# Level 3 of a wavelet convolution with fewer matmuls, up-sampling with high and low halves stacked, and the residual sum earlier on VectorE

## The reference

```python
x = x + _L0_conv_ref(_gn(x), w_qkv, w_proj, gamma, beta)
x = x + _L1_conv_ref(_gn(x), base_w, base_b, base_scale, wconv_w, wscale)

def _L1_conv_ref(x, base_w, base_b, base_scale, wconv_w, wscale):
    cur = x
    for i in range(3):                 # WT_LEVELS
        co = haar2d(cur)               # 4 coefficient planes at half the size
        cur = co[:, :, 0]
        flat = dwconv(co.reshape(B, C * 4, h, w), wconv_w[i]) * wscale[i]   # 5 x 5 depthwise
        level_coeffs.append(flat.reshape(B, C, 4, h, w))
    next_ll = zeros_like(level_coeffs[-1][:, :, 0])
    for i in reversed(range(3)):
        co = level_coeffs[i].at[:, :, 0].add(next_ll)
        next_ll = ihaar2d(co)          # twice the size
    return dwconv(x, base_w) * base_scale + base_b + next_ll
```

## Time and profile before

| | |
|---|---|
| time, median of 3 runs | 11314.09 us (11312.22 to 11319.58) |
| the profiled execution | 11311.75 us, of which its span 11309.9 us |
| PE busy | 10853.3 us (96%) |
| DVE busy | 9314.2 us (82%) |
| ACT busy | 6979.7 us (62%) |
| POOL busy | 3419.9 us (30%) |
| mean granted TensorE clock | 0.992 of full speed |

### The profile page before, as it was taken

One profiled execution on the slowest core, in us unless ns is written; L12 is line 12 of the kernel. 1 busy time (PEld: TensorE's weight loads), 2 busy tenths in 40 slices (PEclk: granted clock), 3 DMA queues, 4 the chain that ended last, 5 costly groups with the idle time before them and its releaser, 6 DMA issues.

```text
span 11309.9 us, 208798 instructions
## 1 busy us (share of the span) xinstructions
PE 10853.3 (96%) x68772; PEld 9284.1 (82%) x68772; DVE 9314.2 (82%) x16092; ACT 6979.7 (62%) x11660; POOL 3419.9 (30%) x2756
## 2 busy tenths in 40 slices
PE   4999999999999999999599999999999999999999
PEld 4888888888888888888588888888888888888888
DVE  6989999899998989988677777777777777777777
ACT  4777777777777777788445445454454545545454
POOL 3444444344444444444222122212222122221221
PEclk9999999999999999999799999999999999999999
DMA  5333233233333333222266666666666766667665
GB/s 184 126 101 125 96 123 123 92 129 101 114 114 116 113 101 130 93 80 81 73 140 151 148 148 147 145 153 147 149 145 145 154 146 150 144 146 153 145 150 118
DMA packets 1149039, 1453.41 MB, mean 129 GB/s; under 512 B 201567, under 2 KB 1111199, under 8 KB 1111455
## 3 DMA queue, kind: packets, MB, share of 16 engines
q1 hardware_dynamic: 1147231, 1442.74, 50.1%
q10 hardware_dynamic: 1376, 6.13, 0.1%
HBM read 1040.06 MB, written 408.56 MB: 128 GB/s over the span
## 4 chain that ended last, share of the span: by engine, by line
PE 49%; DVE 1%; SPq 0%; DMA 0%; issue 0%; POOL 0%; DVEq 0%; POOLq 0%
PE ps_w L1274 10%; PE ps_w L1275 10%; PE ps_w L1276 10%; PE ps_ll L1282 4%; PE ps L1274 4%; PE ps L1275 4%; PE ps L1276 4%; PE ps_w L1317 4%; DVE ob L1399 0%; DVE x L1337 0%; DMA yb<-y_scratch 0%; SPq L1101 0%; SPq L1110 0%; DMA prm<-params 0%; SPq L1120 0%
## 5 line engine op out<-in xcount | busy, mean ns | idle before, releaser
L1274 PE MATMUL ps_w<-zb,mat 128*128 128x512 f32 x4800 | 1925.7, 401 | 1.6 <-DVE ob L1399 1.6
L1276 PE MATMUL ps_w<-zb,mat 128*128 128x512 f32 x4800 | 1907.6, 397 | 0.0
L1275 PE MATMUL ps_w<-zb,mat 128*128 128x512 f32 x4800 | 1907.2, 397 | 0.0
L1227 ACT ACTIVATE z<-x,prm 64x384 f32<-64x384 f32 (+1 forms) x3072 | 1807.2, 659 | 55.5 <-DVE x L1337 47.8
L635 POOL CAST xn_hi<-xs 96x512 fp32r<-96x512 f32 x1024 | 842.7, 823 | 3106.9 <-PE ps_qkv L660 2255.4
L1173 POOL CAST mat<-raw 128x1280 fp32r<-128x1280 f32 (+1 forms) x288 | 344.8, 1215 | 4454.8 <-DMA raw<-vec 2674.2
L1399 DVE SCALAR_TENSOR_TENSOR ob<-ps_w,prm,x 64x512 f32<-64x512 f32 x1920 | 1440.6, 750 | 148.7 <-PE ps_w L1317 109.5
L1337 DVE SCALAR_TENSOR_TENSOR x<-yb,prm,xb 128x1024 f32<-128x1024 f32 (+1 forms) x576 | 1120.4, 1997 | 421.6 <-DMA prm<-params 374.9
L658 PE MATMUL ps_qkv<-wqkv_hi,xn_hi 96*128 96x288 f32 x4096 | 1388.4, 339 | 38.0 <-POOL xn_lo L637 19.8
L637 POOL TENSOR_TENSOR xn_lo<-xs,xn_hi 96x512 fp32r<-96x512 f32 x1024 | 1363.7, 1332 | 81.9
L1247 ACT ACTIVATE ll<-ps_ll 128x512 f32<-128x512 f32 x192 | 115.1, 599 | 1880.5 <-PE ps_ll L1282 1880.5
(11 more groups left out here) (183 smaller groups left out, 24815.2 us busy)
## 6 DMA issues: line engine op xcount, KB each, us to landing
xst<-in_x SPq DMA_DIRECT2D x96, 2048.0 KB, 13.8
xs<-in_x SPq DMA_DIRECT2D x128, 1536.0 KB, 8.9
y_scratch<-ys SPq DMA_DIRECT2D x128, 1536.0 KB, 9.5
out<-ob SPq DMA_DIRECT2D x768, 208.0 KB
xb<-in_x SPq DMA_DIRECT2D x576, 256.0 KB
yb<-y_scratch SPq DMA_DIRECT2D x576, 256.0 KB
raw<-vec SPq DMA_DIRECT2D x192, 320.0 KB, 5.4
raw<-vec SPq DMA_DIRECT2D x384, 160.0 KB, 4.2
```

Source lines behind the costliest of these rows:

```text
L1227: last = nc.scalar.activation(z[q * WROWS:(q + 1) * WROWS, ts, b, :], x1[slot(k, g)][rows, pairs, b, q::2], ACT.Identity, scale=prm[k][row ...
L1274: mm(out_, w[HI], xx[HI], start=start, stop=False)
L1275: mm(out_, w[HI], xx[LO], start=False, stop=False)
L1276: return mm(out_, w[LO], xx[HI], start=False, stop=stop)
```

## The change

- Level 3 on PE: the high and the low part of its input lie side by side in one tensor `in3_hl`. One matmul with the high weights takes both (256 columns, into both halves of `ps_3[:, s]`), a second one with the low weights takes the high part (128 columns). It is 20 matmuls instead of 30. ACT then copies all of `ps_3` (512 columns, not 128) and DVE adds the two halves (`sum3`) ahead of `up3`, whose inputs lie both in SBUF now.
- Up-sampling on PE: the high and the low part of `next_ll` lie on top of each other over the 128 partitions, `next_a` for the upper 64 rows and `next_b` for the lower. Windows 0 and 1 need `next_a` alone, 3 and 4 `next_b` alone, window 2 both: 6 matmuls instead of 10. ACT and DVE write each part in two instructions of 64 partitions.
- `make_x1` stands ahead of `trailing` on DVE.
- The factor of `make_x1` comes from a tensor of its own, `gain`, loaded by a DMA of its own behind the loads of a channel's first set. `prm` is loaded ahead of `raw` on SP; ACT `norm` and DVE `finish` wait for it.
- In the earlier stages three small tensors are given back sooner; nothing that runs there changes.

```diff
@@ wavelet stage, SyncE
+                def load_gain(c, k):
+                    sp.dma_start(gain[k][:], bass.AP(tensor=par_dram.tensor, offset=c * NPAR, ap=[[0, 128], [1, 1]])
+                                 ).then_inc(gain_in[k], 16)
-                def group(m, k, g, fetch=True):
+                def group(m, k, g, fetch=True, more=True):
                     if fetch:
                         m3, k3, g3 = ahead(m, k, g, 3)
                         sp.wait_ge(x1_ready, m * (4 * PAIRW) + (2 * k + g + 3) * PAIRW)
                         sp.sem_inc(sp_turn, 1)
                         load(m3 * 2 + k3, g3)
+                        if g == 0 and more:
+                            load_gain(m * 2 + (k + 2), k)
                     store(m * 2 + k, g, m * 4 + (2 * k + g))
...
                         for g in range(SETS):
                             group(m, k, g)
-                            if g == 1:
-                                sp.wait_ge(mat23_ready, m * 2 + (k + 2))
-                                load_raw(m * 2 + (k + 2))
                         load_prm(m * 2 + (k + 2), k)
+                        sp.wait_ge(mat23_ready, m * 2 + (k + 2))
+                        load_raw(m * 2 + (k + 2))
@@ ScalarE
                     act.wait_ge(l3_ready, qn + 1)
-                    nc.scalar.activation(s3[:], ps_3[:, 0, 0:IMGS * HALF // 4], ACT.Copy).then_inc(s3_copied, 1)
+                    nc.scalar.activation(s3[:].rearrange("p s h n -> p (s h n)"), ps_3[:].rearrange("p s n -> p (s n)"),
+                                         ACT.Copy).then_inc(s3_copied, 1)
                     act.wait_ge(next_ready, qn + 1)
-                    nc.scalar.activation(next_p[HI][:], next_ll[:].rearrange("p n c -> p (n c)"), ACT.Copy
-                                         ).then_inc(next_hi, 1)
+                    both = next_ll[:].rearrange("p n c -> p (n c)")
+                    nc.scalar.activation(next_a[0:64, :], both[0:64], ACT.Copy).then_inc(next_hi, 1)
+                    nc.scalar.activation(next_b[64:128, :], both[64:128], ACT.Copy).then_inc(next_hi, 1)
@@ TensorE
-                    level(ps_3, mat3, in3_p, HALF // 4).then_inc(l3_ready, 1)
+                    for s in range(2):
+                        for d in range(TAPS):
+                            both = (ps_3[:, s, :], mat3[HI][:, s, d, :], in3_hl[:, :, s, :, d:d + HALF // 4])
+                            high = (ps_3[:, s, 0:IMGS * HALF // 4], mat3[LO][:, s, d, :],
+                                    in3_hl[:, HI, s, :, d:d + HALF // 4])
+                            if d == TAPS - 1:
+                                mm(*high, start=False, stop=False)
+                            last = mm(*both, start=d == 0, stop=d == TAPS - 1)
+                            if d < TAPS - 1:
+                                mm(*high, start=False, stop=False)
+                    last.then_inc(l3_ready, 1)
...
                     for t in range(WINDOWS):
-                        for h in (HI, LO):
-                            last = mm(ps_w[t][:], up_sb[:, t, :], next_p[h][:], start=False, stop=h == LO)
+                        upper, lower = t < UPPER, t >= WINDOWS - LOWER
+                        if upper:
+                            last = mm(ps_w[t][:], up_sb[:, t, :], next_a[:], start=False, stop=not lower)
+                        if lower:
+                            last = mm(ps_w[t][:], up_sb[:, UPPER + t - (WINDOWS - LOWER), :], next_b[:], start=False,
+                                      stop=True)
                         last.then_inc(win_ready, 1)
@@ VectorE
                     dve.wait_ge(s3_copied, qn + 1)
-                    v.tensor_tensor(up3[:, :, 0], s3[:], ps_3[:, 1, 0:n], ALU.add)
+                    v.tensor_tensor(sum3[:], s3[:, :, 0], s3[:, :, 1], ALU.add).then_inc(s3_summed, 1)
+                    dve.wait_ge(s3_summed, qn + 1)
+                    v.tensor_tensor(up3[:, :, 0], sum3[:, 0], sum3[:, 1], ALU.add)
...
+                    v.tensor_tensor(next_a[64:128, :], both[0:64], next_a[0:64, :].bitcast(F32), ALU.subtract)
+                    dve.wait_ge(next_hi, qn * 2 + 2)
+                    v.tensor_tensor(next_b[0:64, :], both[64:128], next_b[64:128, :].bitcast(F32), ALU.subtract
+                                    ).then_inc(next_lo, 1)
...
                         finish(qn - 1, mb, kb, gb_, range(2, WINDOWS))
+                    if n is None or n + 2 < GROUPS_C:
+                        make_x1(*ahead(m, k, g, 2))
                     if n is None or n + 1 < GROUPS_C:
                         trailing(qn + 1, ahead(m, k, g, 1)[2])
                     up_levels(qn)
                     split_next(qn)
-                    if n is None or n + 2 < GROUPS_C:
-                        make_x1(*ahead(m, k, g, 2))
```

More of the change, by code:

```diff
@@ L1023, in wt_attention_kernel @@
             prm = [sb_(f"prm_{k}", [128, NPAR]) for k in range(2)]
+            gain = [sb_(f"gain_{k}", [128, 1]) for k in range(2)]
             down_sb = sbr_("down_sb", [128, WINDOWS, HALF])
-            up_sb = sbr_("up_sb", [128, WINDOWS, 2 * WROWS])
+            UPPER = -(-(HALF // 2) // (OROWS // 2))
+            LOWER = WINDOWS - HALF // OROWS
+            up_sb = sbr_("up_sb", [128, UPPER + LOWER, 2 * WROWS])
             inside_sb = sb_("inside_sb", [128, PAIRW])
@@ L1033, in wt_attention_kernel @@
             in2_p = [sbr_(f"in2_{h}", [128, 2, IMGS, HALF // 2 + 4]) for h in range(2)]
-            in3_p = [sbr_(f"in3_{h}", [128, 2, IMGS, HALF // 4 + 4]) for h in range(2)]
-            next_p = [sbr_(f"next_{h}", [128, IMGS * HALF]) for h in range(2)]
-            s3 = sb_("s3", [128, IMGS * HALF // 4])
+            in3_hl = sbr_("in3_hl", [128, 2, 2, IMGS, HALF // 4 + 4])
+            in3_p = [in3_hl[:, h] for h in range(2)]
+            next_a, next_b = (sbr_(f"next_{h}", [128, IMGS * HALF]) for h in "ab")
+            s3 = sb_("s3", [128, 2, 2, IMGS * HALF // 4])
+            sum3 = sb_("sum3", [128, 2, IMGS * HALF // 4])
             up3 = sb_("up3", [128, IMGS * HALF // 4, 2])
@@ L1053, in wt_attention_kernel @@
             x1_ready = sem_("x1_ready")
+            gain_in = [sem_(f"gain_in{k}") for k in range(2)]
             ll_ready, ll_copied, in2_ready, in3_ready = (sem_(n) for n in ("ll_ready", "ll_copied", "in2_ready", "in3_ready"))
@@ L1376, in up_levels @@
                     dve.wait_ge(s3_copied, qn + 1)
-                    v.tensor_tensor(up3[:, :, 0], s3[:], ps_3[:, 1, 0:n], ALU.add)
-                    v.tensor_tensor(up3[:, :, 1], s3[:], ps_3[:, 1, 0:n], ALU.subtract).then_inc(up3_ready, 1)
+                    v.tensor_tensor(sum3[:], s3[:, :, 0], s3[:, :, 1], ALU.add).then_inc(s3_summed, 1)
+                    dve.wait_ge(s3_summed, qn + 1)
+                    v.tensor_tensor(up3[:, :, 0], sum3[:, 0], sum3[:, 1], ALU.add)
+                    v.tensor_tensor(up3[:, :, 1], sum3[:, 0], sum3[:, 1], ALU.subtract).then_inc(up3_ready, 1)
                     dve.wait_ge(l2_ready, qn + 2)
@@ L1387, in split_next, with finish @@
                 def split_next(qn):
-                    dve.wait_ge(next_hi, qn + 1)
-                    v.tensor_tensor(next_p[LO][:], next_ll[:].rearrange("p n c -> p (n c)"), next_p[HI][:].bitcast(F32),
-                                    ALU.subtract).then_inc(next_lo, 1)
-                def finish(qn, k, g, ts):
+                    both = next_ll[:].rearrange("p n c -> p (n c)")
+                    dve.wait_ge(next_hi, qn * 2 + 1)
+                    v.tensor_tensor(next_a[64:128, :], both[0:64], next_a[0:64, :].bitcast(F32), ALU.subtract)
+                    dve.wait_ge(next_hi, qn * 2 + 2)
+                    v.tensor_tensor(next_b[0:64, :], both[64:128], next_b[64:128, :].bitcast(F32), ALU.subtract
+                                    ).then_inc(next_lo, 1)
+                def finish(qn, mc, k, g, ts):
                     for t in ts:
@@ L1408, in steps @@
                     before = n is None or n > 0
-                    kb, gb_ = (1 - k, 1) if g == 0 else (k, 0)
+                    mb, kb, gb_ = ahead(m, k, g, -1)
                     if before:
-                        finish(qn - 1, kb, gb_, (0,))
+                        finish(qn - 1, mb, kb, gb_, (0,))
                     make_in(qn)
                     if before:
-                        finish(qn - 1, kb, gb_, (1,))
+                        finish(qn - 1, mb, kb, gb_, (1,))
                     split_in(qn)
                     if before:
-                        finish(qn - 1, kb, gb_, range(2, WINDOWS))
+                        finish(qn - 1, mb, kb, gb_, range(2, WINDOWS))
+                    if n is None or n + 2 < GROUPS_C:
+                        make_x1(*ahead(m, k, g, 2))
                     if n is None or n + 1 < GROUPS_C:
@@ L1421, in steps @@
                     split_next(qn)
-                    if n is None or n + 2 < GROUPS_C:
-                        make_x1(*ahead(m, k, g, 2))
                 dve.wait_ge(const_in, 48)
```

(8 more changed lines are left out.)

28 lines of the change are left out of this document (16 added, 12 removed).

## The result

The changed kernel takes 11158.65 us (median of 4 runs, 11156.94 to 11163.67) against 11314.94 us before: a ratio of 0.986, interval 0.985 to 0.988. The forecast was 11085 us, with a range up to 11150. The direction was right and the size was not: 156 us were gained where 229 were forecast, and the time lies 9 us outside the range.

What follows compares the result with a forecast made beforehand. TensorE (PE), busy throughout the wavelet stage, was taken to set the pace. 11311.75 - 184 (level 3) - 46 (up-sampling) + 1 (gain issues) = 11083 us; with the median 2.3 above the profiled execution, forecast 11085 us, range 11045 to 11150.

Steps and rivals of the forecast that it cites:

- Level 3: Level 3 on PE: 20 matmuls instead of 30 save 0.96 us a group, 184 us in all (159 to 211).
- Rival 3: Level 3 on PE: columns set the price, so only the up-sampling's 46 us are left: 11267 us; chance 0.04.
- Up-sampling: Up-sampling on PE: four matmuls go, but PE waits 0.70 us for window 0's finish; 0.24 of 0.94 us gained, 46 us.
- Rival 4: Group boundary: all the up-sampling's 0.94 us comes through because window 0's finish is quicker; 135 us more, 10950; chance 0.04.
- make_x1, gain, the loads: DVE, SP and DMAs: make_x1 falls into DVE's idle time, worth nothing by itself; gain issues cost 1 us at stage start.
- With POOL: DVE beside GpSimd's building: subtractions hold DVE's last two, next_b's ends near C + 23.2; PE at C + 26.2, 3 us left.
- rival 2: DVE held by POOL: sum3 and up3 held by one subtraction each lose up to 77 us: 11160 us; chance 0.07.

Runs made afterwards that it cites:

- e5: The changed kernel with level 3 as before (30 matmuls of 128 columns, no sum3): 11272.46 us, ratio 0.9967 to the kernel before.
- e2: The changed kernel, but GpSimd starts building mat2 and mat3 only behind VectorE's split_next: 11089.94 us, ratio 0.981 to the kernel before.
- e4: As e1, with window 0's up-sampling matmul and the wait for next_lo ahead of sum_down on TensorE: 10973.40 us, ratio 0.970 to the kernel before.
- e8: The kernel of e4, with GpSimd building mat2 and mat3 behind split_next as in e2: 10924.21 us, ratio 0.966 to the kernel before.
- e6: The kernel before with only make_x1 ahead of trailing, gain loaded by itself and prm ahead of raw: 11314.46 us, ratio 1.0004.
- e7: The changed kernel, but make_x1 takes its factor from prm and waits for it, gain gone: 11155.59 us, ratio 0.986 to the kernel before.
- e3: The changed kernel with make_x1 back at the end of VectorE's group: 11588.49 us, ratio 1.024 to the kernel before.
- e1: The changed kernel, but sum3 and up3 keep one input in PSUM, ScalarE copying only ps_3's high halves: 11089.31 us, ratio 0.980 to the kernel before.

## Why the prediction was wrong

- **Level 3**: right. Forecast 0.96 us a group, measured 0.97 (e5 against e2). Rival 3, by which columns set the price, falls.
- **Up-sampling**: right in mechanism and nearly in size. Forecast 0.24 of 0.94 us, measured 0.20 (e5); e4 and e8 show that the rest was held back by `finish` of window 0. With that wait away a group is 0.85 us shorter (e8 against e2), 0.15 more than the 0.70 of the prediction; where these 0.15 us come from no run shows. Rival 4 falls with it.
- **make_x1, gain, the loads**: right. Cost and gain none (e6, e7); `make_x1` takes 3.66 us now that no work of GpSimd lies beside it. That it stands early is needed all the same: at its old place behind the new, longer and held chain it costs 430 us, part of it by the lower clock (e3 against the changed kernel).
- **The step that failed** is the paragraph "With POOL", where `next_lo` was put at C + 23.2 with 3 us to spare. It let GpSimd hold an instruction only beside its subtractions, and took its casts as harmless. The casts hold too: the last instruction of `trailing` by 1.00 us and `sum3` by 1.05. By these 2 us `up3` slid from ahead of the first subtraction to beside both, one instruction each, 5.4 us more, and `next_lo` stood at C + 26.8 where PE wanted it at C + 26.2. The end is the one that rival 2 priced, "only if `sum3` and `up3` are held by one each", at C + 26.4 to 27 and 11160 us with a chance of 0.07; 11158.65 came. But rival 2 had subtractions alone hold, and named nothing that would make VectorE late first; the casts did that. No run moves the casts without the subtractions, so their share is read from the rows and not from an experiment of its own; that GpSimd's building as a whole is the cause is shown by e2. Without the hold the sum nearly holds: e1 and e2 give 11089 us, 4 us beside the forecast (221 us gained against the kernel before on their chip, where 229 were forecast).
- The trace of before had shown it, in the stage's first group, where a cast met `trailing`. GpSimd, then VectorE, in the kernel before:

```profile
5652.89 0.92 POOL L1173 CAST mat<-raw 128x640 fp32r<-128x640 f32 x1 [47.24 <-DMA raw<-vec]
```

```profile
5653.15 1.21 DVE L1353 TENSOR_TENSOR zb<-z,zb 128x512 fp32r<-128x512 f32 x1
```

  It takes 0.69 elsewhere. The cast was over at 5653.81, GpSimd's subtraction began at 5653.99, and alone VectorE's instruction would have ended at 5653.84: it was the cast that held it. In the steady groups before, the last instruction of `trailing` had started 0.16 us ahead of the cast, and the two overlapped by 0.6 us:

```profile
8042.72 0.75 DVE L1350 SCALAR_TENSOR_TENSOR zb<-z,mask,zb 128x512 fp32r<-128x512 f32 x1
```

```profile
8042.88 1.69 POOL L1173 CAST mat<-raw 128x1280 fp32r<-128x1280 f32 x1 [18.81 <-PE ps L1276]
```

  VectorE's instruction kept its 0.75 us, and it was the cast that grew: 1.69 us, where the two together take 2.89 and so the second about 1.2. The cost was there, on the engine where it didn't matter. With level 3 shorter, the casts start at C + 13.55 instead of C + 14.49, while `trailing` starts at C + 11.9 as before (0.06 us later, not the 0.25 of the prediction). Its last instruction now starts 0.83 us behind the cast, at 8035.74, and takes 1.74 us. The prediction wrote down both shifts, but not that they turn round who comes first.
- The chances were wrong as well. Rival 2's condition was 2 us of delay in a chain that had just been given two instructions open to a hold; 0.07 for it, and a range that ended 10 us below its price, said that the margin was known better than it was.

## What to carry to other kernels

A shared resource costs nothing in a profile as long as its users take turns: when a change moves two engines against each other, lay their instructions over one another again at the new times, each short one that may be held too, and don't take a wait's price from the old overlap. On VectorE an input left in PSUM, or GpSimd's work put where VectorE idles, was worth 65 to 69 us here, beside the 156 that the change brings by itself. And when matmuls are taken from a place where another engine is level with TensorE, work that doesn't depend on it belongs in between (e4): that gave 116 us (e1 to e4), where the four matmuls removed there had given 0.20 x 192 = 38.

## What the runs showed of the hardware

- GpSimd's casts, with one SBUF input, hold VectorE's instructions with two SBUF inputs as its subtractions do: 0.74 to 1.74 us and 0.42 to 1.47, while instructions with one PSUM and one SBUF input beside the same casts keep their 0.29 us (e1). The casts become longer as well, 3.68 us for two beside VectorE's held instructions and 2.89 in the earlier trace rows.
- Not every instruction beside a cast is held: in the kernel before, the one that had started 0.16 us ahead of the cast kept its 0.75 us and the cast took 1.69; in the changed kernel the third L1383, started at 8035.13 during the cast of 2.02 us, kept its 0.68, and L1380 behind it took 1.74.
- One short VectorE instruction is held until about the end of the GpSimd instruction under way, and the next one again by the following: 0.29 us became 2.94 and 3.01.
- A wait of PE of 3.5 us brought the granted clock to 0.50 (e3); those of 0.5 us in every group of the changed kernel left it at 1.00.
